# No row picking on TensorE in a graph layer's gather phase: GpSimd gathers all 46 rows of a round, and the histogram's operands get eight buffers

## The chip, the cores and the metric

One Trainium2 chip, one of its cores. The metric is the device time of one execution in microseconds (us), the median of the runs shown.

## What is computed

A graph layer followed by a mixture-of-experts feed-forward layer, both residual, on x of 6250 rows by 256 columns, in float32, with 200,000 edges sorted by their target node `dst`. Cut to the part that the change is in:

```
h    = batch_norm(layernorm(x) @ w1.T + b1)
diff = h[src] - h[dst]                    # 200,000 rows of 256
m    = segment_max(diff, dst)             # one row for each node
hg   = gelu(batch_norm(concat(h, m) @ wg.T + bg))
x    = x + batch_norm(hg @ w2.T + b2) + layernorm(x)
x    = x + experts(layernorm(x))          # 8 experts, three 256x256 layers each
```

Since `h[dst]` is the same for all edges of a node, `m` comes from the maximum of the gathered rows `h[src]` over each run of equal `dst`. So the middle of the kernel gathers 200,000 rows of 1 KB each and takes a running maximum over them.

## The kernel before

The edges are dealt out so that each of the 128 partitions holds 1564 consecutive edges. A step handles one edge of each partition, 128 rows; 46 steps make a round and 34 rounds make the gather phase. A round has seven groups of 7, 7, 7, 7, 6, 6 and 6 steps (`GS`). The rows of a round lie in `ring`, one slot for each step.

**The gather.** GpSimd (POOL) issues one indirect DMA for each step, line 648. Before each group it waits until the store of the same group of the round before has landed (`s_st`), and before every fourth gather until the running maximum is at most 21 steps behind (`s_ch`, `LEAD`). In rounds 1 to 32 it gathers 42 steps only (`by_pool`).

**The picks.** The last four steps of rounds 1 to 32 are made on TensorE (PE). The row numbers of the next round are broadcast to all partitions (SP, line 757, tile `ids`) and copied to PSUM (ACT, line 690). For each of 49 tiles of 128 nodes a one-hot matrix of 128 by 512 is built: four of seven by ScalarE (ACT) in two instructions (lines 670 and 675), three of seven by VectorE (DVE, line 821). PE multiplies the two halves of the node table, high and low part, with it: four matmuls of 512 columns (lines 999 and 1001). `picks_out`, `turn_back` and `result` turn the sum and write it into `ring[:, 42:46]`. Seven buffers `oh` hold the one-hot matrices; PE gives them back with `s_ohf`.

**The running maximum.** DVE does one instruction for each step, line 815, on `ring`, each waiting for the one before (`s_ch`). At a group's first step it waits for that group's gathers (`s_g`), at step 42 for the picks (`s_pe`). SP stores each finished group to `runs` (line 762).

**The histogram.** In rounds 0 to 31 each group also counts how many edges each node has: DVE builds two one-hot operands (`low_hots`, line 827, after the fourth step, and `high_hots`, line 832, after the fifth), and PE multiplies them in seven small matmuls (`counts`, line 970), the last of which increments `s_cnt`. There is one buffer of each operand, so `low_hots` first waits for the `counts` of the group before. The counts end with `s_c1`.

**Around it.** In rounds 0 to 15 SP also fetches pieces of the expert weights (`part`), ACT and DVE split them (lines 679 and 837), SP writes them back. Rounds 32 and 33 have no picks and no counts: there PE, ACT and DVE begin the first half of the second matmul (`columns`, line 1039, and `sums`, lines 189 to 191, 14 pieces; ACT takes them out in lines 724 and 730), while POOL and DVE finish the chain. DVE stops in round 32 after its first group for a product of PE (line 1059, read at line 911) and for what follows from the counts. The stage ends when the last of the 14 pieces is out.

Of the kernel before, what the change touches and what calls it, by code (L numbers as in the profile page):

```python
# [19 lines left out]
F32 = mybir.dt.float32  # L20
# [7 lines left out]
P = 128  # L28
N = 6250
C = 256  # L30
# [20 lines left out]
NPE = 4  # L51
PSLOT = STEPS - NPE
PG = ROUNDS - 2
SLOTS = 7
LEAD = 21
BD = (1, 3, 5)
BA = (0, 2, 4, 6)
# [15 lines left out]
assert NCH * TPC == NT and WIN * P >= E and (P - 1) * WIN < E and HR * HCOL >= WIN and HR == 4 * NE == PG and PG * NPE == P and SLOTS * NG == NT  # L73
# [23 lines left out]
def build(nc, io):  # L97
    ctx = ExitStack()
    with ctx:
# [15 lines left out]
        srcT_d = nc.dram_tensor("srcT_d", (PG, NPE * P), F32, kind="Internal").ap()  # L115
# [117 lines left out]
        places = sub(free0, ("zT", MAT), ("gT", 2 * MAT), ("ring", 0), ("src", WIN * 4), ("pen", WIN * 4), ("oh", SLOTS * NPE * P * 4),  # L233
# [28 lines left out]
        def h0_of(c):  # L262
# [7 lines left out]
        p2 = sub(places["free"], ("lo16", HR * HCOL * 2), ("hi16", HR * HCOL * 2), ("oh_lo", NG * P * 2), ("oh_hi", NG * NT * 2), ("ids", 2 * NPE * P * 4 + 512),  # L270
                 ("cnt", 6 * NT * 4), ("zr", P * 2), ("rowi", 2 * P * 4), ("rowf", 2 * P * 4), ("node", NT * 4), ("nodef", NT * 4),
                 ("nodeneg", NT * 4), ("fixi", 64), ("tri", P * 4), ("ones", P * 4))
        lo16 = plan.at("lo16", [P, HR * HCOL], BF16, p2["lo16"])
        hi16 = plan.at("hi16", [P, HR * HCOL], BF16, p2["hi16"])
        oh_lo = plan.at("oh_lo", [P, NG, P], BF16, p2["oh_lo"])
        oh_hi = plan.at("oh_hi", [P, NG, NT], BF16, p2["oh_hi"])
# [9 lines left out]
        nodef = plan.at("nodef", [P, NT], F32, p2["nodef"])  # L286
        nodeneg = plan.at("nodeneg", [P, NT], F32, p2["nodeneg"])
        dst_i = plan.at("dst_i", [P, WIN], I32, places["oh"])
        dig_i = plan.at("dig_i", [P, WIN], I32, places["part"])
        assert WIN * 4 <= SLOTS * NPE * P * 4 and WIN * 4 <= PW * 4 + 4096  # L290
# [5 lines left out]
        assert 6272 >= WIN * 4 and 6272 + 3 * C * 4 + P * 4 <= SLOTS * NPE * P * 4  # L296
# [277 lines left out]
        oh = plan.at("oh", [P, SLOTS, NPE * P], F32R, places["oh"])  # L574
        ids = plan.at("ids", [P, 2, NPE * P], F32, p2["ids"])
        srcf = plan.at("srcf", [P, PG * NPE], F32, places["part_hi"] + P * 4)
        part = plan.at("part", [P, PW], F32, places["part"])
        part_hi = plan.at("part_hi", [P, PW], F32R, places["part_hi"])
        srcTs = plan.at("srcTs", [P, P], F32, places["part"])
        accT = plan.at("accT", [P, KC, NPE * P], F32, places["part"] + PW * 4)  # L580
# [19 lines left out]
        s_ids, s_ch, s_oh, s_cnt = sem("s_ids"), sem("s_ch"), sem("s_oh"), sem("s_cnt")  # L600
        s_accS, s_back = sem("s_accS"), sem("s_back")
        s_ohd, s_oha, s_ohf, s_ab, s_pe, s_acc0, s_idp = sem("s_ohd"), sem("s_oha"), sem("s_ohf"), sem("s_ab"), sem("s_pe"), sem("s_acc0"), sem("s_idp")
        s_tt, s_tst, s_tev, s_zh, s_zl, s_srcf, s_srcT, s_srcS, s_srcD = sem("s_tt"), sem("s_tst"), sem("s_tev"), sem("s_zh"), sem("s_zl"), sem("s_srcf"), sem("s_srcT"), sem("s_srcS"), sem("s_srcD")
# [5 lines left out]
        ND, NA = NG * len(BD), NG * len(BA)  # L609
# [15 lines left out]
        def turned(n):  # L625

            return 4 if n < 2 else 2

        def by_pool(i, g):

            return GS[g] - (NPE if g == NG - 1 and 1 <= i <= PG else 0)

        def gathered(i, g):

            return 16 * sum(by_pool(j, g) for j in range(i + 1))

        with nc.Block() as block:

            @block.gpsimd
            def _(pool):  # L640
                for i in range(ROUNDS):
                    for g in range(NG):
                        if i:
                            pool.wait_ge(s_st[g], 16 * i)
                        for k in range(GO[g], GO[g] + by_pool(i, g)):
# [7 lines left out]
            def _(act):  # L653
                def picks_out(i):

                    two = (4, 2)[i % 2]
                    act.wait_ge(s_acc0, i + 1)
                    act.activation(accT[:].rearrange("p k n -> p (k n)"), banks(two, 2), ACT.Copy).then_inc(s_accS, 1)

                def result(i):  # L660

                    two = (4, 2)[(i - 1) % 2]
                    act.wait_ge(s_st[NG - 1], 16 * i)
                    act.wait_ge(s_ch, STEPS * i + 1)
                    act.wait_ge(s_back, i)
                    act.activation(ring[:, PSLOT:STEPS, :].rearrange("p s n -> p (s n)"), banks(two, 2), ACT.Copy).then_inc(s_pe, 1)

                def distance(i, h, g, v):
                    wait(act, s_ohf, NT * i + SLOTS * g + v + 1)
                    act.activation(oh[:, v, :], ids[:, bass.ds(h, 1), :].rearrange("p a n -> p (a n)"), ACT.Abs,  # L670
                                   bias=nodeneg[:, bass.ds(SLOTS * g + v, 1)]).then_inc(s_ab, 1)

                def one_hot(i, g, j, v):
                    wait(act, s_ab, NA * i + len(BA) * g + j + 1)
                    act.activation(oh[:, v, :], oh[:, v, :].bitcast(F32), ACT.Relu, bias=ones[:, 0:1], scale=-1.0).then_inc(s_oha, 1)  # L675

# [4 lines left out]
                def hots(i, h, g):  # L681
                    distance(i, h, g, BA[0])
                    for j in range(1, len(BA)):
                        distance(i, h, g, BA[j])
                        one_hot(i, g, j - 1, BA[j - 1])
                    one_hot(i, g, len(BA) - 1, BA[-1])
# [6 lines left out]
                def body(i, h, piece):  # L693
                    hots(i, h, 0)
                    if i:
                        picks_out(i - 1)
# [1293 lines left out]
```

## Time and profile before

| | |
|---|---|
| runs | 3648.39, 3649.25, 3667.12 us; median 3649.25 |
| span of the profiled execution | 3634.8 us; about 14 us of its time lie outside the span, if it ran as the median |
| gather phase, first gather's start to last gather's end | 98.7 to 2441.4 us |
| its last round, with 46 gathers | from 2382.2 us |
| end of the stage that follows it | 2524.7 us |

"Busy" is the time in which an engine executed an instruction. An idle time is put down to the instruction whose signal ended it; "remote" means that the signal came at a time that fits no recorded end of an instruction, and "issue" that no wait is to be seen. PEclk is the granted TensorE clock as a share of 2.4 GHz.

### The profile page before, as it was taken

What the parts mean: (1) busy time and instruction counts of PE and PEld (TensorE: products, weight loads), DVE (VectorE), ACT (ScalarE), POOL (GpSimd) and SP (SyncE); (2) the same over time, 40 slices, a digit from 0 to 9 for tenths busy, and PEclk for the clock granted to TensorE, in tenths of its full rate; (3) what the DMA queues carried; (4) which work ended last, traced back from release to release, by engine and by line L of the source; (5) the groups of instructions that cost most, each with busy time, mean ns of one, the idle gap of its engine ahead of it and who ended that gap; (6) DMA issues with size and microseconds to landing.
All of it is one profiled execution on the core that took longest, in us unless ns stands there. A gap on an engine that the chain in (4) does not pass through costs nothing. (4 is left out here: it accounts for less than half of the span.)

```text
span 3634.8 us, 41575 instructions
## 1 busy us (share of the span) xinstructions
PE 2966.5 (82%) x15504; PEld 2461.7 (68%) x15504; DVE 2207.0 (61%) x4089; ACT 1962.2 (54%) x2741; POOL 1496.1 (41%) x1530
## 2 busy tenths in 40 slices
PE   6578777787877778788887777728988999999998
PEld 5456565665665656566665666527878999999998
DVE  6576666666666666666666666540885556555544
ACT  5356555555555655555555555415165565566554
POOL 1566565565666655556665555561410000000000
PEclk9789898898898998889898898868999999999999
DMA  7355555555555555455555555450213324333331
GB/s 227 114 195 196 181 197 187 194 197 182 194 191 189 189 169 170 167 169 181 170 183 169 171 176 171 160 204 25 61 75 98 118 105 135 128 115 115 115 109 69
DMA packets 164927, 559.97 MB, mean 154 GB/s; under 512 B 31190, under 2 KB 68374, under 8 KB 157556
## 3 DMA queue, kind: packets, MB, share of 16 engines
q1 hardware_dynamic: 87492, 355.23, 26.1%
q0 software_dynamic: 77232, 202.08, 19.5%
q8 instruction: 122, 2.00, 0.2%
q14 instruction: 81, 0.66, 0.1%
HBM read 320.19 MB, written 237.00 MB: 153 GB/s over the span
## 5 line engine op out<-in xcount | busy, mean ns | idle before, releaser
L648 POOL DMA_INDIRECT ring<-runs,src_i x1436 | 1410.4, 982 | 1004.2 <-DVE ring L815 518.7
L999 PE MATMUL ps<-oh,zhl 128*128 128x512 f32 x3136 | 1347.5, 430 | 321.9 <-issue 159.7
L1001 PE MATMUL ps<-oh,zhl 128*128 128x512 f32 x3136 | 1308.0, 417 | 12.8 <-issue 12.5
L670 ACT ACTIVATE oh<-ids,nodeneg 128x512 fp32r<-128x512 f32 x896 | 633.6, 717 | 900.7 <-PE ps L1001 487.4
L999 PEld LDWEIGHTS ps<-oh,zhl 128*128 128x128 f32 x3136 | 642.1, 205 | 515.2 <-issue 186.4
L815 DVE SCALAR_TENSOR_TENSOR ring<-ring,pen 128x256 f32<-128x256 f32 x1564 | 750.4, 480 | 63.5 <-DMA ring<-runs,src_i 32.3
L821 DVE TENSOR_SCALAR oh<-ps,nodef 128x512 fp32r<-128x512 f32 x672 | 501.7, 747 | 403.6 <-PE ps L1001 248.5
L1001 PEld LDWEIGHTS ps<-oh,zhl 128*128 128x128 f32 x3136 | 643.2, 205 | 146.1 <-issue 15.3
L675 ACT ACTIVATE oh<-oh,ones 128x512 fp32r<-128x512 f32 x896 | 613.6, 709 | 0.0
L827 DVE TENSOR_TENSOR oh_lo<-lo,ps 128x896 bf16<-128x896 bf16 x224 | 242.8, 1084 | 328.7 <-remote 302.3
L1569 ACT ACTIVATE av<-ps,vecs 128x896 f32<-128x896 f32 x224 | 246.3, 1100 | 330.4 <-PE ps L191 330.4
L1717 DVE TENSOR_TENSOR h2l<-av,h2h 128x896 fp32r<-128x896 f32 x112 | 122.3, 1092 | 203.4 <-ACT h2h L1571 203.4
L1724 DVE SCALAR_TENSOR_TENSOR y<-ps,wv,y 128x256 f32<-128x256 f32 x392 | 168.9, 479 | 109.6 <-PE ps L1917 109.0
L1915 PE MATMUL ps<-fw,h2h 128*128 128x256 f32 x784 | 224.4, 286 | 3.3 <-DVE h2l L1717 3.3
L1916 PE MATMUL ps<-fw,h2l 128*128 128x256 f32 x784 | 221.8, 283 | 0.0
L1917 PE MATMUL ps<-fw,h2h 128*128 128x256 f32 x784 | 221.5, 282 | 0.0
L970 PE MATMUL ps<-oh_hi,oh_lo 128*128 128x49 bf16 x1575 | 85.4, 190 | 128.2 <-DVE oh_hi L832 69.4
L970 PEld LDWEIGHTS ps<-oh_hi,oh_lo 128*128 128x128 bf16 x1575 | 61.4, 99 | 180.6 <-issue 82.5
L1497 POOL DMA_DIRECT2D y<-in_x x5 | 8.4, 1671 | 415.6 <-DMA y<-res_d 415.6
L189 PE MATMUL ps<-h1h,fw 128*128 128x512 f32 x448 | 167.3, 374 | 1.9 <-DVE h1l L1717 1.9
L1717 DVE TENSOR_TENSOR h1l<-av,h1h 128x896 fp32r<-128x896 f32 x112 | 121.8, 1088 | 75.0 <-ACT h1h L1571 75.0
L191 PE MATMUL ps<-hnh,fw 128*128 128x512 f32 x448 | 164.6, 367 | 0.0
(294 smaller groups left out, 3872.2 us busy)
## 6 DMA issues: line engine op xcount, KB each, us to landing
runs<-ring SPq DMA_DIRECT2D x136, 896.0 KB
fw<-wsp SPq DMA_DIRECT2D x56, 1536.0 KB, 6.5
runs<-ring SPq DMA_DIRECT2D x102, 768.0 KB
ring<-runs,src_i POOLq DMA_INDIRECT x1436
ids<-srcT_d SPq DMA_DIRECT2D x32, 256.0 KB
res_d<-x_all SPq DMA_DIRECT2D x7, 896.0 KB
y<-res_d SPq DMA_DIRECT2D x7, 896.0 KB, 7.0
part<-in_Wx SPq DMA_DIRECT2D x16, 384.0 KB
```

What stands on the lines that cost most here:

```text
L648: pool.indirect_dma_start(ring[:, k, :], None, runs[0:N, :], bass.IndirectOffsetOnAxis(ap=src_i[:, STEPS * i + k:STEPS * i + k + 1], axis= ...
L670: act.activation(oh[:, v, :], ids[:, bass.ds(h, 1), :].rearrange("p a n -> p (a n)"), ACT.Abs, bias=nodeneg[:, bass.ds(SLOTS * g + v, 1)]) ...
L675: act.activation(oh[:, v, :], oh[:, v, :].bitcast(F32), ACT.Relu, bias=ones[:, 0:1], scale=-1.0).then_inc(s_oha, 1)
L815: dve.scalar_tensor_tensor(out=ring[:, k, :], in0=ring[:, before, :], scalar=pen[:, STEPS * i + k:STEPS * i + k + 1], in1=ring[:, k, :], o ...
L821: dve.tensor_scalar(oh[:, v, :], ps[:, bass.ds(6 + h, 1), :].rearrange("p a n -> p (a n)"), nodef[:, SLOTS * g + v:SLOTS * g + v + 1], Non ...
L827: dve.tensor_tensor(oh_lo[:], lo16[:, bass.ds(at, NG)].unsqueeze(2).to_broadcast([P, NG, P]), io_lo.unsqueeze(1).to_broadcast([P, NG, P]), ...
L999: pe.matmul(ps[:, two + k, :], z_hi(g)[:, v, cols], oh[:, v, :], start=g == 0 and v == 0, stop=False, skip_group_check=True)
L1001: r = pe.matmul(ps[:, two + k, :], z_lo(g)[:, v, cols], oh[:, v, :], start=False, stop=False, skip_group_check=True)
L1569: act.activation(av[:, m, :], block_banks(m), ACT.Relu, bias=dv(bi, 2 * e + m), scale=dv(sc, 2 * e + m)).then_inc(s_ev, 1)
L1717: dve.tensor_tensor(lo[:, m, :], av[:, m, :], hi[:, m, :].bitcast(F32), ALU.subtract).then_inc(s_hl6, 1)
L1915: pe.matmul(o, h2h[:, k, st], fw[:, b, 0, 2, k, :], start=k == 0, stop=False)
L1916: pe.matmul(o, h2l[:, k, st], fw[:, b, 0, 2, k, :], start=False, stop=False)
```

## The change

The picks are taken out: the one-hot matrices, the broadcast row numbers, their DMAs and semaphores, the copies into `ring`. POOL gathers 46 steps in every round. What PE still does in rounds 0 to 31 is `counts`. Their two operands have eight buffers, partly in the place of `oh` and `ids`: `low_hots` of group t waits for the `counts` of group t - 8. ACT's start on the following stage waits for `s_c1`, and so does SP's load of its weights (line 798 and its neighbour), which had waited for the last pick.

```
-NPE = 4
-PSLOT = STEPS - NPE
+NSET = 8
...
-        def by_pool(i, g):
-            return GS[g] - (NPE if g == NG - 1 and 1 <= i <= PG else 0)
...
                 def chain(i, k):
...
-                    if k == PSLOT and 1 <= i <= PG:
-                        dve.wait_ge(s_pe, i)
...
-                def one_hot(i, h, g, v):
-                    wait(dve, s_ohf, NT * i + SLOTS * g + v + 1)
-                    dve.tensor_scalar(oh[:, v, :], ps[:, bass.ds(6 + h, 1), :].rearrange("p a n -> p (a n)"),
-                                      nodef[:, SLOTS * g + v:SLOTS * g + v + 1], None, ALU.is_equal).then_inc(s_ohd, 1)
...
                 def low_hots(i, g):
-                    wait(dve, s_cnt, NG * i + g + 1)
+                    t = NG * i + g + 1
+                    if t >= NSET:
+                        wait(dve, s_cnt, t - NSET + 1)
...
                         if first:
                             row_low(g)
-                        chain(i, k)
-                        one_hot(i, h, g, BD[0])
-                        chain(i, k + 1)
-                        one_hot(i, h, g, BD[1])
-                        chain(i, k + 2)
-                        one_hot(i, h, g, BD[2])
-                        chain(i, k + 3)
+                        for j in range(4):
+                            chain(i, k + j)
                         low_hots(i, g)
...
-                for i in range(PG):
-                    picked(i)
-                counts(NG * HR)
-                turn_back(PG - 1)
+                for t in range(NG * HR + 1):
+                    counts(t)
...
-                rounds(body)
+                for i in range(2 * NE):
+                    high(i)
...
                 act.wait_ge(s_xs, 32 * 2 * NE)
+                act.wait_ge(s_c1, 1)
...
                 sp.wait_ge(s_xs, 32 * 2 * NE)
-                sp.wait_ge(s_acc0, PG)
+                sp.wait_ge(s_c1, 1)
```

## Rows read from the trace of the kernel before

**Rows 1.** The page, part 1: busy time, share, instructions of each engine.
```profile
PE 2966.5 (82%) x15504; PEld 2461.7 (68%) x15504; DVE 2207.0 (61%) x4089; ACT 1962.2 (54%) x2741; POOL 1496.1 (41%) x1530
```

**Rows 2.** Windows: round 0, rounds 1-31, round 32, round 33, PE's rest.
```profile
core 0: us, PE busy (x) PEld busy (x) DVE busy (x) ACT busy (x) POOL busy (x), PEclk, DMA share, GB/s
98.60:183.70 85.10, 50.75 (x235) 38.51 (x234) 55.35 (x110) 36.87 (x49) 48.46 (x46) 0.74 0.36 114
183.70:2303.10 2119.40, 1669.16 (x7890) 1290.39 (x7889) 1370.70 (x2526) 1198.87 (x1840) 1275.72 (x1302) 0.89 0.54 182
2303.10:2382.10 79.00, 53.55 (x247) 43.95 (x245) 39.77 (x90) 27.11 (x43) 40.77 (x42) 0.76 0.47 158
2382.10:2441.60 59.50, 9.02 (x32) 8.20 (x33) 27.97 (x58) 3.12 (x6) 45.48 (x46) 0.54 0.67 231
2441.60:2524.60 83.00, 75.02 (x424) 67.20 (x422) 2.91 (x6) 51.60 (x92) 0.00 (x0) 0.96 0.06 21
```

**Rows 3.** The gathers, line 648: durations, and what ended POOL's idle time.
```profile
L648 POOL DMA_INDIRECT ring<-runs,src_i x1436: 951/957/2510, 98.7 to 2440.4; - x180
...
  DVE ring L815: 518.7, 177
```

**Rows 4.** Waits in rounds 1 to 31: total, times, longest.
```profile
POOL ring L648 <- DVE ring L815: 464.8, 162, 6.1
...
DVE oh_lo L827 <- remote: 302.3, 63, 8.8
DVE oh L821 <- PE ps L1001: 239.4, 108, 9.4
```

**Rows 5.** Timeline around a pause of POOL: start, duration, engine, instruction, idle before.
```profile
895.92 0.34 PE L970 MATMUL ps<-oh_hi,oh_lo 128*128 128x49 bf16 x7
...
903.20 0.95 POOL L648 DMA_INDIRECT ring<-runs,src_i  x1 [0.30 <-issue]
906.53 1.09 DVE L827 TENSOR_TENSOR oh_lo<-lo,ps 128x896 bf16<-128x896 bf16 x1 [8.77 <-remote]
906.59 1.33 ACT L670 ACTIVATE oh<-ids,nodeneg 128x512 fp32r<-128x512 f32 x2 [4.89 <-remote]
...
910.11 0.95 POOL L648 DMA_INDIRECT ring<-runs,src_i  x1 [5.96 <-DVE ring L815]
```

**Rows 6.** The page, part 5: groups of instructions that the change removes.
```profile
L999 PE MATMUL ps<-oh,zhl 128*128 128x512 f32 x3136 | 1347.5, 430 | 321.9 <-issue 159.7
...
L670 ACT ACTIVATE oh<-ids,nodeneg 128x512 fp32r<-128x512 f32 x896 | 633.6, 717 | 900.7 <-PE ps L1001 487.4
...
L821 DVE TENSOR_SCALAR oh<-ps,nodef 128x512 fp32r<-128x512 f32 x672 | 501.7, 747 | 403.6 <-PE ps L1001 248.5
```

**Rows 7.** Timeline, DVE: a histogram pair, and the chain in round 33.
```profile
890.33 1.07 DVE L827 TENSOR_TENSOR oh_lo<-lo,ps 128x896 bf16<-128x896 bf16 x1
...
891.73 0.50 DVE L832 TENSOR_TENSOR oh_hi<-hi,ps 128x343 bf16<-128x343 bf16 x1
...
2411.77 3.63 DVE L815 SCALAR_TENSOR_TENSOR ring<-ring,pen 128x256 f32<-128x256 f32 x7 [5.22 <-DMA ring<-runs,src_i]
```

**Rows 8.** Timeline, DVE and POOL in round 32.
```profile
2359.86 0.16 DVE L911 TENSOR_TENSOR vecs<-vecs,ps 128x4 f32<-128x4 f32 x1 [22.44 <-PE ps L1059]
...
2369.13 1.08 POOL L648 DMA_INDIRECT ring<-runs,src_i  x1 [18.79 <-DVE ring L815]
```

**Rows 9.** Timeline, ACT in round 33: the next stage under unbroken gathers.
```profile
2390.55 1.09 ACT L724 ACTIVATE zs<-ps 128x512 fp32r<-128x512 f32 x2 [10.00 <-remote]
2402.50 0.58 ACT L730 ACTIVATE gT<-ps,vecs 128x384 f32<-128x384 f32 x1 [10.87 <-issue]
2419.99 0.58 ACT L730 ACTIVATE gT<-ps,vecs 128x384 f32<-128x384 f32 x1 [16.91 <-remote]
2436.82 0.87 ACT L724 ACTIVATE zs<-ps 128x384 fp32r<-128x384 f32 x2 [16.25 <-issue]
2448.08 1.05 ACT L730 ACTIVATE gT<-ps,vecs 128x384 f32<-128x384 f32 x2 [10.39 <-remote]
```

More of the change, by code:

```diff
@@ L623, in piece_of @@
             return n // 2, a, w
-        def turned(n):
-            return 4 if n < 2 else 2
-        def by_pool(i, g):
-            return GS[g] - (NPE if g == NG - 1 and 1 <= i <= PG else 0)
         def gathered(i, g):
-            return 16 * sum(by_pool(j, g) for j in range(i + 1))
+            return 16 * GS[g] * (i + 1)
         with nc.Block() as block:
@@ L644, in _ @@
                             pool.wait_ge(s_st[g], 16 * i)
-                        for k in range(GO[g], GO[g] + by_pool(i, g)):
+                        for k in range(GO[g], GO[g + 1]):
                             if (k - GO[g]) % 4 == 0 and STEPS * i + k > LEAD:
@@ L653, in _ @@
             def _(act):
[L654 to L675, printed above, removed]
                 def high(i):
@@ L679, in high @@
                     act.activation(part_hi[:], part[:], ACT.Copy).then_inc(s_xh, 1)
[L681 to L686, printed above, removed]
-                def numbers(i, h):
-                    wait(act, s_ids, 16 * i + 16)
-                    act.activation(ps[:, bass.ds(6 + h, 1), :].rearrange("p a n -> p (a n)"),
-                                   ids[:, bass.ds(h, 1), :].rearrange("p a n -> p (a n)"), ACT.Copy).then_inc(s_idp, 1)
[L693 to L696, printed above, removed]
-                    if i < PG - 1:
-                        if i:
-                            wait(act, s_ohd, ND * i)
-                        numbers(i + 1, 1 - h)
-                    hots(i, h, 1)
-                    if piece is not None:
-                        high(i)
-                    hots(i, h, 2)
-                    if i:
-                        result(i)
-                    for g in range(3, NG):
-                        hots(i, h, g)
-                act.wait_ge(s_srcT, 1)
-                act.activation(srcTs[:], ps[:, 6, 0:P], ACT.Copy).then_inc(s_srcS, 1)
                 for c in range(NCH):
@@ L775, in body @@
                 def body(i, h, piece):
-                    first = isinstance(i, int) and i == 0
-                    if not (isinstance(i, int) and i == PG - 1):
-                        wait(sp, s_ids, 16 * i + 16)
-                        if not first:
-                            wait(sp, s_oha, NA * i)
-                        columns(i + 1, 1 - h)
                     if piece is not None:
@@ L866, in body @@
                     first = isinstance(i, int) and i == 0
-                    wait(dve, s_idp, i + 1)
                     for g in range(NG):
```

107 lines of the change are left out of this document (23 added, 84 removed).

## The prediction

> **What bounds the kernel now.** I read the page first: PE is busy for 82% of the span [rows 1], which would make the picks the thing to remove. But a share over the whole span says little, so I next asked for windows by round. Rounds 1 to 31 take 2119.4 us, 68.4 us each. In them PE is busy 1669 us of 2119, DVE 1371, ACT 1199, POOL 1276 [rows 2]: four engines at 57 to 79%, none of them full. Such a stretch is bound by how they wait for each other, and so the third view was the waits. The reader is to see a ring in it: POOL waits 465 us for the running maximum, and DVE waits 302 us before `low_hots` and 239 us before its one-hot matrices [rows 4], both for signals of PE.
>
> The fourth view, the timeline around one such wait, shows that PE is not late with its work. The seven matmuls of `counts` start at 895.92 and take 0.34 us in all. DVE, which needs nothing but their signal, starts at 906.53, ten us later, and so does ACT at 906.59. What happened between is that POOL, after a row of back-to-back gathers, ended its last one at 904.15 and stood still [rows 5]. I read this as: while POOL issues gathers without a break, signals of PE come late, and when POOL stops they all come, 2.4 us later in these rows. POOL then waits on for DVE's next steps, 5.96 us in all, and the circle begins again. A place without picks shows the same. In round 33 POOL gathers 46 times in 59.5 us without a pause [rows 2], and ACT, which takes out sums that PE has long finished, gets its signals one at a time at 2390.55, 2402.50, 2419.99, 2436.82 and, with POOL done at 2441.4, the next at 2448.08 [rows 9]. From 2390.55 to 2436.82 these are three intervals of 15.4 us on the mean; with the waits of 10.00 and 10.39 us at both ends, about 13.5 to 14 us.
>
> So the gather phase is bound by POOL's gathers plus the pauses in which PE's signals catch up. 42 gathers at 1275.72 / 1302 = 0.980 us, with 0.30 us between two of them [rows 2, 5], make 53.8 us; the other 14.6 us of a round are pauses: POOL's waits for DVE alone are 464.8 / 31 = 15.0 us a round, the longest 6.1 us [rows 4].
>
> **What is removed.** 3136 matmuls of line 999 and as many of line 1001, 896 distances and 896 one-hots on ACT, 672 one-hots on DVE [rows 6], the turning back, the broadcast of the row numbers on SP. None of this is paid for on POOL, so its 1348 us of PE or 502 us of DVE are no terms of the sum. What it is worth is that DVE and ACT no longer wait for PE 49 times in a round.
>
> **What is added.** Four gathers in each of 32 rounds. For the cost of a round of 46 there is a direct measurement, round 33: 59.5 us with 46 chain steps and seven stores beside them, DMA share 0.67 [rows 2]. The other end is the median gather, 46 x (0.957 + 0.30) = 57.8 us [rows 3, 5]. I take 59.5, since there DVE works beside it as it will; 57.8 would be worth another 53 us over 31 rounds.
>
> DVE does not become the bound: seven chain steps take 3.63 us, a histogram pair 1.07 and 0.50 us [rows 7]. A round is 46 x 0.52 + 7 x 1.57 = 35 us of 59.5. Nor does the DMA: in round 33 DVE waits 5.2 us for a group's gathers and then has 3.6 us of work [rows 7], 8.9 us for 7 steps, which is POOL's pace; POOL waits for no landing at all. Stores hold nothing up either: the view of [rows 4] has no wait of POOL for one, and with POOL at most 24 of 46 steps ahead a group's store has 15 steps, about 19 us, to land. SP loses work and gains none.
>
> **Eight buffers.** `low_hots` still needs PE's signal, now that of eight groups back. A group lasts 59.5 x 7 / 46 = 9.05 us, so the signal may be 7 x 9.05 = 63 us late. PE gives one signal in 9.05 us; if unbroken gathers let through one in 14 us [rows 9], the queue grows by 1/9.05 - 1/14 = 0.039 a us and reaches seven after about 180 us. From then on DVE goes at one group in 14 us, POOL at one in 9.05; POOL has about 12 steps of its 21 to spare and loses 3.8 in each group, so it pauses some 45 us later. The pause is that of [rows 5], 6 us: the signals all come, DVE makes four steps, POOL goes on. That is 6 us in each 230, in rounds 1 to 31 eight pauses, 48 us. The ends: nothing, if the queue is emptied in time after all; and one pause after each seven groups and the 12 spare steps, 63 + 15 us and the pause itself, every 84 us, if unbroken gathers let nothing through: 22 pauses, 132 us. I take 48, because [rows 9] is the only stretch with the new pace, and things went through there.
>
> The Trainium skill (TensorE: Matmul & The Clock Gate, "The cost: per-tile semaphore tail") gives 26.3 ns for each increment. By it the signals would never be late, the eight buffers would be worth nothing, and the sum would have 0 here. The ten us in [rows 5] are against it; the time it gives is the first rival's.
>
> **The sum**, on the span. Round 0: DVE's chain of it starts when the statistics before it are done, which the change doesn't touch; POOL waits for that as before. DVE saves its 21 one-hots, POOL's own 46 gathers stay: 82 for 85.1. Rounds 1 to 31: 31 x 59.5 = 1844.5 for 2119.4. Round 32: four gathers more, 5 us, on 79.0 [rows 2]. Its pause of 18.79 us [rows 8] stays, since DVE waits for a product of PE that POOL's gathers delay; SP loads the weights for it only after `s_c1` now, which was not so, but the signal comes in the pause as before. 84. Round 33: 59.5. Pauses: 48. Together 2118 for 2343.1, that is 225 us less. What follows (83.0 us, PE busy 75 of them [rows 2]) keeps its length: the pieces that PE could finish during rounds 32 and 33 are held up by the gathers now as before. The profiled span is 3634.8, the median 3649.25, about 14 us outside it that stay: 3649 - 225 = 3424.
>
> **Rivals.** *No pauses* (chance 0.20): one signal in 9 us gets through. For it: even now, with PE sending eight signals in each group, DVE was held for a late one at `low_hots` 63 times in 217 groups [rows 4], not each time. Against: [rows 9], where one came in 14 us. It gives 3649 - 273 = 3376, and with the fast gathers 3325.
>
> *Nothing gets through* (0.15): 22 pauses of 6 us, 3649 - 273 + 132 = 3508; if the signals take the 6.7 us to come that they took after POOL's last gather [rows 9], a pause is 10 us and the time 3596.
>
> *Slower than before* (0.04): DVE's chain holds up POOL's descriptor work. The chain's instruction has both inputs in SBUF, and if POOL stood still for all of its 0.48 us, a round would be 57.8 + 46 x 0.48 = 80 us, 31 x (80 - 68.4) = 360 us more than before, some 4010 us; it ends slower from 68.4 us a round on, that is when 0.23 us of each chain step hold POOL up. The Trainium skill (SBUF — State Buffer, "Who interferes with whom") says that a DVE instruction with two SBUF inputs and a GpSimd instruction that reads SBUF block each other fully. Round 33 is against it: 46 chain steps, and the 46 gathers beside them took 45.48 us, 0.989 each against the median of 0.957 [rows 2, 3], so 0.03 us of a step, not 0.48.
>
> *No change* (0.02): the pauses stay as they are, 14.6 us a round, and the four gathers add 5 us, which the shorter round 0 does not pay; this would need DVE to wait for each `counts` signal, which eight buffers exclude as long as a signal is under 63 us late.
>
> My own case has 0.59, with a range of its own of 3375 to 3470. The range for 8 in 10 goes from the middle of the first rival to the middle of the second: 3345 to 3520. Faster by over 0.5% (18 us, about what a measurement of this kernel can tell): 0.94; within 0.5%: 0.02; slower: 0.04.
>
> **What the profile after should show.** 1564 gathers, mean 0.98 to 0.99 us. Rounds 1 to 31 of 60 to 62 us. POOL's waits for DVE in these rounds, 465 us before, at 40 to 60, in few pieces of 3 to 6 us each, one in about four rounds, and before each of them DVE waiting at `low_hots` for 10 us or more for a signal of PE that was finished long ago. DVE waiting 4 to 6 us in each group for gathers. PE's granted clock mostly at the lower of its levels, 1.2 GHz, as in round 33 (0.54 of 2.4 GHz [rows 2]). A gather phase of about 2118 us, the stage after it 83 us as before.
>
> **What would make this wrong.** If DVE's waits at `low_hots` are gone, the first rival holds and the time is below 3400. If they come once or twice in a round, the second. If gathers take over 1.1 us with DVE busy, the third. If round 32's pause grows beyond 19 us, because `s_c1` stands behind up to seven late signals and the load of the weights and ACT's work behind it, the time is up to 20 us above the sum.

## The result and the profile after

The changed kernel takes 3532.84 us, the median of four runs (3531.34 to 3536.09), against 3648.82 us before (four runs, 3645.08 to 3667.12). The ratio is 0.9685, with a 95% interval of 0.966 to 0.971: 3.2% faster. I had predicted 3424 us, a gain of 225; the gain is 116, about half, and the time lies 13 us above my range. The profiled execution took 3531.3 us with a span of 3529.6, 105 less than before.

The engines' busy times, from the page, to be laid beside [rows 1]:

```profile
PE 1400.1 (40%) x8911; PEld 1223.8 (35%) x8911; DVE 1811.5 (51%) x3414; ACT 733.2 (21%) x852; POOL 1632.1 (46%) x1658
```

1566 us of PE's busy time and 1229 of ACT's are gone, and the span gave back 105. The windows by stage, to be laid beside [rows 2]: round 0, rounds 1 to 31, round 32, round 33, and what PE still does after.

```profile
core 0: us, PE busy (x) PEld busy (x) DVE busy (x) ACT busy (x) POOL busy (x), PEclk, DMA share, GB/s
97.60:180.00 82.40, 23.80 (x131) 17.03 (x130) 53.33 (x101) 11.72 (x10) 50.81 (x46) 0.56 0.38 121
180.00:2196.90 2016.90, 158.16 (x1533) 96.61 (x1533) 994.22 (x1889) 12.64 (x15) 1406.54 (x1426) 0.50 0.59 195
2196.90:2277.70 80.80, 23.29 (x112) 20.47 (x113) 29.05 (x71) 10.06 (x18) 45.07 (x46) 0.56 0.48 158
2277.70:2336.80 59.10, 10.37 (x34) 8.57 (x32) 22.49 (x46) 2.61 (x5) 44.94 (x46) 0.56 0.64 212
2336.80:2420.00 83.20, 74.23 (x418) 66.80 (x418) 2.91 (x6) 50.99 (x91) 0.00 (x0) 0.92 0.05 20
```

Four of the five rows are within 3.2 us of their terms (82, 84, 59.5, 83). All of the miss is in one: rounds 1 to 31 take 2016.9 us, 65.1 a round, where 1844.5 + 48 = 1892.5 were forecast. The gathers are not to blame; line 627, the view of one line:

```profile
L627 POOL DMA_INDIRECT ring<-runs,src_i x1564: 947/953/2697, 97.6 to 2335.5; - x196
```

The median is 953 ns and the mean in rounds 1 to 31 1406.5 / 1426 = 0.986 us. So POOL was busy for 1406.5 us, 1426 x 0.30 = 428 is the step from one gather to the next [rows 5], and the remaining 182 us are pauses. I had 48 on top of 59.5 us a round, and on that base it is 2016.9 - 1844.5 = 172. The waits of these rounds, to be laid beside [rows 4], show their shape:

```profile
POOL ring L627 <- issue: 414.8, 1296, 3.8
DVE ring L722 <- remote: 315.2, 170, 3.1
...
DVE oh_lo L731 <- remote: 200.4, 25, 15.1
DVE ring L722 <- issue: 173.2, 115, 7.0
DVE ring L722 <- DMA ring<-runs,src_i: 151.1, 42, 6.6
POOL ring L627 <- DVE ring L722: 134.7, 105, 8.7
DVE ring L722 <- DVE ring L722: 132.0, 177, 1.3
POOL ring L627 <- remote: 60.9, 25, 4.2
```

POOL's waits for DVE and for signals of no known origin are 134.7 + 60.9 = 196 us, where I had forecast 40 to 60. DVE still waits at `low_hots` (`oh_lo`, line 731), 25 times, up to 15.1 us; the one signal that this line of the kernel waits for is PE's. New is the running maximum, line 722: it waits for its own step before, hundreds of times and up to 3.1 us, where the chain of [rows 7] had a step each 0.52 us. DVE's timeline in two stretches, before and after signals began to come late (a line with x4 is four steps in a row):

```profile
227.44 2.11 DVE L722 SCALAR_TENSOR_TENSOR ring<-ring,pen 128x256 f32<-128x256 f32 x4
229.46 1.08 DVE L731 TENSOR_TENSOR oh_lo<-lo,ps 128x896 bf16<-128x896 bf16 x1
...
324.26 0.48 DVE L722 SCALAR_TENSOR_TENSOR ring<-ring,pen 128x256 f32<-128x256 f32 x1 [0.85 <-DVE ring L722]
325.66 0.48 DVE L722 SCALAR_TENSOR_TENSOR ring<-ring,pen 128x256 f32<-128x256 f32 x1 [0.92 <-DVE ring L722]
327.06 0.48 DVE L722 SCALAR_TENSOR_TENSOR ring<-ring,pen 128x256 f32<-128x256 f32 x1 [0.92 <-DVE ring L722]
327.46 1.08 DVE L731 TENSOR_TENSOR oh_lo<-lo,ps 128x896 bf16<-128x896 bf16 x1
...
333.44 0.48 DVE L722 SCALAR_TENSOR_TENSOR ring<-ring,pen 128x256 f32<-128x256 f32 x1 [2.39 <-remote]
335.46 0.48 DVE L722 SCALAR_TENSOR_TENSOR ring<-ring,pen 128x256 f32<-128x256 f32 x1 [1.54 <-remote]
```

In the second stretch a step of 0.48 us comes every 1.4 us and more. `low_hots` at 327.46, which needs nothing of the step before, starts 0.40 us after that step: instructions reach DVE in time, and only what waits for the step before is late. DVE falls behind, and POOL, which looks before every fourth gather whether it is at most 21 steps ahead, stands still for it:

```profile
327.30 1.08 POOL L627 DMA_INDIRECT ring<-runs,src_i  x1 [2.50 <-DVE ring L722]
...
334.09 0.95 POOL L627 DMA_INDIRECT ring<-runs,src_i  x1 [3.06 <-remote]
```

In round 32 POOL's one pause, for the chain that DVE had left [rows 8], is now 22.05 us, where it was 18.79; the round is still 3 us shorter than I had it.

### The profile page after: what moved, and what is told of

Its sections match the earlier page's. It is cut to its first block and busy times, and to the rows that moved or that the text cites. A ratio compares the mean times of both kernels' runs of the same rounds, so it can differ in the third digit from the quotient of the medians.

```text
span 3529.6 us, 25757 instructions
## 1 busy us (share of the span) xinstructions
PE 1400.1 (40%) x8911; PEld 1223.8 (35%) x8911; DVE 1811.5 (51%) x3414; ACT 733.2 (21%) x852; POOL 1632.1 (46%) x1658
## 5 line engine op out<-in xcount | busy, mean ns | idle before, releaser
L627 POOL DMA_INDIRECT ring<-runs,src_i x1564 | 1547.4, 989 | 763.5 <-issue 454.1
L864 PE MATMUL ps<-oh_hi,oh_lo 128*128 128x49 bf16 x1575 | 160.9, 214 | 1903.5 <-issue 1302.0
L864 PEld LDWEIGHTS ps<-oh_hi,oh_lo 128*128 128x128 bf16 x1575 | 98.6, 113 | 1965.8 <-issue 1345.2
L649 ACT ACTIVATE zs<-ps 128x512 fp32r<-128x512 f32 (+1 forms) x56 | 27.4, 541 | 1177.0 <-remote 1166.3
L635 ACT ACTIVATE part_hi<-part 128x768 fp32r<-128x768 f32 x16 | 13.5, 842 | 945.2 <-DMA part<-in_Wx 762.8
L184 PE MATMUL ps<-h1h,fw 128*128 128x512 f32 x448 | 167.4, 374 | 1.9 <-DVE h1l L1570 1.9
L185 PE MATMUL ps<-hnl,fw 128*128 128x512 f32 x448 | 164.5, 367 | 0.0
L186 PE MATMUL ps<-hnh,fw 128*128 128x512 f32 x448 | 164.4, 367 | 0.0
L186 PE MATMUL ps<-h1h,fw 128*128 128x512 f32 x448 | 164.0, 366 | 0.0
L185 PE MATMUL ps<-h1l,fw 128*128 128x512 f32 x448 | 163.7, 365 | 0.0
L184 PE MATMUL ps<-hnh,fw 128*128 128x512 f32 x448 | 163.5, 365 | 0.0
L1768 PEld LDWEIGHTS ps<-fw,h2h 128*128 128x128 f32 x784 | 150.8, 192 | 4.3 <-DVE h2l L1570 3.7
```

Source lines behind the costliest of these rows:

```text
L184: pe.matmul(out, wh, xh, start=first and i == 0, stop=False)
L185: pe.matmul(out, wh, xl, start=False, stop=False)
L186: r = pe.matmul(out, wl, xh, start=False, stop=last and i == n - 1)
L627: pool.indirect_dma_start(ring[:, k, :], None, runs[0:N, :], bass.IndirectOffsetOnAxis(ap=src_i[:, STEPS * i + k:STEPS * i + k + 1], axis= ...
L864: r = pe.matmul(ps[:, 0, 0:NT], oh_lo[t % NSET][:, n, :], oh_hi[t % NSET][:, n, :], start=False, stop=False, skip_group_check=True)
L1768: pe.matmul(o, h2h[:, k, st], fw[:, b, 0, 2, k, :], start=k == 0, stop=False)
```

## The experiments

All times are medians of four or more runs, beside runs of the kernel before on the same chip. That matters here, since the 18 experiments fell on six chips, and the kernel before is not the same on them: 3077.7, 3081.7 and 3079.3 us on three of them (called 3080 chips below), 3639.9, 3593.9 and 3651.0 on the other three (3640 chips; the result above, 3648.8, is of their kind). Some edits ran on both kinds; each repeat has a label of its own.

**Four kernels that each undo or lighten a part (e1 to e4).** e1 has one buffer for the histogram's operands:

```
-NSET = 8
+NSET = 1
```

> The kernel after with one buffer for the histogram's operands in place of eight, so only the picks are taken out. Theory A (signals are late while POOL gathers without a break, and eight buffers absorb part of that): DVE stands at low_hots in nearly each group until POOL has paused, some 15 us of pauses on 59.5 us a round as before, 31 x (74 - 65) = 280 us more than the 3533 us of the kernel after, about 3800. Rival B (the buffers are worth nothing, taking the picks out is the whole gain): 3533.

e2 is the kernel before, picks kept, with two buffers (eight don't fit beside the picks' tiles):

```
+        NSET = 2
...
-                    wait(dve, s_cnt, NG * i + g + 1)
+                    t = NG * i + g + 1
+                    if t >= NSET:
+                        wait(dve, s_cnt, t - NSET + 1)
```

> The kernel before with two buffers for the histogram's operands in place of one, picks kept (there is no room for more beside them). Theory A: low_hots waits no longer (302 us of waits in the kernel before), but DVE's and ACT's one-hot matrices wait for the same late signals of PE right behind it, so the pauses stay: 3600 to 3649. Rival C (the buffers carry the gain and the picks cost nothing): 3530 to 3560.

e3 is the changed kernel without `counts` on PE, so it leaves out the histogram, and without DVE's wait for it:

```
-                    if t >= NSET:
-                        wait(dve, s_cnt, t - NSET + 1)
...
-                for t in range(NG * HR + 1):
-                    counts(t)
+                wait(pe, s_oh, NG * HR + 1)
```

> The kernel after without the histogram's matmuls: TensorE stands still from round 0 to the end of round 31 and sends no signal; DVE still builds the operands. It leaves out the run-end histogram. Theory A (besides PE's signals also DVE's own come late, so its chain, which waits for its own signal at each step, falls behind): the waits at low_hots go, the slow stretches of the chain stay, only the pauses of over 5 us go, some 50 us in all: about 3480. Rival D (only PE's late signals make pauses): rounds 1 to 31 at 59.5 us, 172 us less, 3361.

e4 has PE signal in each fourth group only; DVE's wait, not shown, counts in fours with it:

```
-                    r.then_inc(s_cnt, 1)
+                    if t % 4 == 3:
+                        r.then_inc(s_cnt, 1)
```

> The kernel after with TensorE signalling only each fourth group of the histogram, eight buffers kept. Theory A with a rate (unbroken gathers let one PE signal through in about 14 us, and one is sent in 36 us here): as with TensorE silent, 3480 to 3500. Rival E (signals are held until POOL pauses, however few they are): DVE stands as often as in the kernel after or oftener, 3533 or more. Rival D: 3361.

All four fell on a 3080 chip, with the kernel before at 3077.7 us, and all my expectations had been written for the other kind. e1 took 3234.0 us (ratio 1.051, interval 1.049 to 1.053), e3 3233.4 (1.050, 1.049 to 1.052), e4 3233.0 (1.050, 1.048 to 1.052), e2 3079.2 (1.001, 1.000 to 1.002). So here every kernel without the picks is 5% slower than the one with them, and neither the buffers nor PE's signals change anything beyond the intervals. Rounds 1 to 31 by windows, first of e4, then of e2 with its 42 gathers:

```profile
166.30:2001.90 1835.60, 103.13 (x1526) 73.65 (x1526) 978.07 (x1877) 12.63 (x15) 1400.91 (x1426) 0.50 0.64 214
```

```profile
164.00:1852.60 1688.60, 1553.80 (x7951) 1230.13 (x7951) 1355.25 (x2542) 1218.33 (x1853) 1291.80 (x1302) 0.96 0.69 229
```

That is 1835.6 / 1426 = 1.287 us for a gather and 1688.6 / 1302 = 1.297: POOL's busy time and 0.30 us between gathers leave 7 and 6 us of these stretches, so the round is POOL's gathers and nothing else, with the picks or without. The transfers are no slower on a 3640 chip: the mean busy time of the DMA engines is 0.64 x 1835.6 = 1175 us in e4 and 0.59 x 2016.9 = 1190 us in the changed kernel. PE makes all its picks in the 54.5 us that POOL needs for 42 gathers. POOL's longest wait in e4 is the ordinary one:

```profile
POOL ring L627 <- issue: 377.4, 1238, 0.3
POOL ring L627 <- DVE ring L722: 57.3, 188, 0.3
```

Taking the picks out therefore costs four gathers a round, 1835.6 - 1688.6 = 147 us of the 3233.0 - 3079.2 = 154 between the two.

**The changed kernel again, and three more (e5 to e8).** They fell on a 3640 chip, the kernel before at 3639.9 us. e5 has no edit.

> The changed kernel, nothing edited. Theory A: it was faster than the kernel before because signals come late while GpSimd gathers without a break, and how late they come is a property of the chip that runs it. Then its time follows the kernel before beside it: if the kernel before takes about 3078 us here, as in the four runs before this one, the changed kernel takes 3225 to 3240 us (ratio about 1.05, no pause of GpSimd in rounds 1 to 31, 58 to 61 us a round); if the kernel before takes about 3649 us, 3520 to 3545 us (0.968, some 66 pauses). Theory B: the four edits tried so far each cost it the same 5%, and the unchanged one is faster than the kernel before on any chip: under 3040 us beside 3078.

3534.0 us, ratio 0.971 (0.967 to 0.975), as in the result. The changed kernel without an edit was never run on a 3080 chip; four variants of it were (e1, e3, e4, e16; e1 and e3 again as e9 and e12), and take 3231 to 3238 us there.

e6 orders the chain by a drain of DVE's pipe, not by its own signal:

```
                     if STEPS * i + k:
-                        dve.wait_ge(s_ch, STEPS * i + k)
+                        dve.drain()
```

> VectorE's chain waits for the previous step by a drain of its own pipe in place of a wait for its own semaphore. Theory A (VectorE's own signals come late after some 60 unbroken gathers): on a chip where the kernel before takes 3649 us, chain steps stay 0.5 us apart, GpSimd no longer pauses for the chain but only where a late signal of TensorE holds VectorE, and rounds 1 to 31 take 60 to 62 us each for 65.1, about 3400 to 3440 us in all. Theory C (the chain is slow since its instructions compete with the gathers for SBUF): the steps stay 1.3 to 3.5 us apart and the time stays 3530. On a chip where the kernel before takes 3078 us nothing is late, so within 10 us of the unchanged kernel by both.

3531.5 us, ratio 0.971 (0.967 to 0.975): nothing. And the steps are as far apart as before, though none waits for a signal; DVE's timeline of e6:

```profile
324.17 0.48 DVE L722 SCALAR_TENSOR_TENSOR ring<-ring,pen 128x256 f32<-128x256 f32 x1 [1.89 <-issue]
325.57 0.48 DVE L722 SCALAR_TENSOR_TENSOR ring<-ring,pen 128x256 f32<-128x256 f32 x1 [0.92 <-issue]
327.65 0.48 DVE L722 SCALAR_TENSOR_TENSOR ring<-ring,pen 128x256 f32<-128x256 f32 x1 [1.60 <-issue]
```

The same 0.92 us stands in front of a step in both kernels. So the chain's own semaphore is not what is late; the step before counts as done late for its successor, whichever way that is asked. Theory A falls in this part. Competition for SBUF (theory C) does not explain it either: the instruction itself keeps its 0.48 us, and in e16 on a 3080 chip the same drains, beside gathers at a faster pace, give four steps in 2.16 us:

```profile
322.37 2.16 DVE L726 SCALAR_TENSOR_TENSOR ring<-ring,pen 128x256 f32<-128x256 f32 x4 [2.93 <-DMA ring<-runs,src_i]
```

e7 stops POOL twice in a round:

```
                                                     ).then_inc(s_g[g], 16)
+                        if g in (2, 6):
+                            pool.wait_ge(s_g[g], gathered(i, g))
```

> GpSimd waits twice in each round, after the third and the seventh group, until that group's own gathers have landed; nothing else is changed. Theory A: with a stop in each 26 us no row of gathers is long enough for signals to fall behind; each stop costs the landing time of the last gather, some 2 us, so 4 us a round. Where the kernel before takes 3649 us: rounds 1 to 31 take 62 to 64 us each, in which all pauses are these stops, in all 3440 to 3510 us, under the unchanged kernel's 3533. Where it takes 3078 us: 4 us a round more than the unchanged kernel, about 3360 us. Theory C: the stops only add, in both cases 100 to 140 us above the unchanged kernel.

3535.2 us, ratio 0.971 (0.967 to 0.976), a round of 2042.9 / 31 = 65.9 us. With the stops nothing is late any more: the view of DVE's waits in rounds 1 to 31 has no line for `low_hots` and none for the step before, only the gathers, and POOL's view has the stops.

```profile
DVE ring L724 <- DMA ring<-runs,src_i: 1011.8, 211, 7.3
DVE ring L724 <- issue: 18.9, 6, 4.5
...
POOL ring L627 <- issue: 427.0, 1310, 5.0
POOL ring L627 <- DMA ring<-runs,src_i: 197.2, 56, 4.4
```

And the time is the same. I had expected either a gain of some 20 to 90 us or a loss of 100 to 140; the stops took the place of the pauses. They last 197.2 / 56 = 3.5 us on the mean. By itself e7 doesn't tell a fixed pace of gathers from a stop that cures the lateness and costs as much: at the 2 us that a stop costs on a 3080 chip (e11 below), its 62 stops would be 124 of its 2042.9 - 1400.4 - 428 = 215 us of pauses.

e8 leaves out one gather in each of four groups, from round 1 on, so POOL issues 42 in a round and no picks are made (those steps work on old rows):

```
+                            if i and g < 4 and k == GO[g + 1] - 1:
+                                continue
```

> Leaves out one gather in each of the first four groups of rounds 1 to 33, the steps then working on rows left from the round before; everything else is that of the changed kernel, so GpSimd issues 42 gathers in a round as the kernel before does, and TensorE picks no rows. Theory A: a gather costs 1.29 us of a round where nothing is late, so with 4 fewer a round takes 54 to 55 us and the whole 33 x 5.1 = 170 us less than the unchanged kernel: about 3065 us where the kernel before takes 3078, that is, the same within 0.6%, since what TensorE and VectorE save there is worth nothing. Theory D (the picks' work cost the kernel before something too, hidden under the same round time): under 3030 us. Where the kernel before takes 3649 us: about 3350 us.

3348.6 us, ratio 0.920 (0.916 to 0.924). Rounds 1 to 31:

```profile
180.50:2024.70 1844.20, 159.60 (x1533) 96.87 (x1533) 993.02 (x1889) 12.64 (x15) 1290.54 (x1302) 0.50 0.60 205
```

1844.2 / 1302 = 1.416 us for a gather; in the changed kernel it was 2016.9 / 1426 = 1.414. This pair splits the change on a 3640 chip: e8 is 3639.9 - 3348.6 = 291 us under the kernel before, and the changed kernel is 3534.0 - 3348.6 = 185 us over e8, 1.40 us for each of 132 gathers. Four of these are in round 33, where the kernel before gathers 46 as well; with them set apart (4 x 1.40 = 6 us, an estimate), taking out the picks, with eight buffers, is worth some 285 us, and the 128 gathers that make up for them take some 180 of it back.

**Meant for a 3640 chip (e9 to e12).** e9, e10 and e12 are e1, e2 and e3 once more; e11 stops POOL once a round (`if g == 6:`).

> The changed kernel with one buffer for the histogram's operands in place of eight, once more, since the first run of it fell on a chip without late signals. Theory A (late signals cost by the pause they make GpSimd take, and pauses come when signals have fallen behind after some 60 gathers, whoever waits): where the kernel before takes about 3640 us, VectorE waits at the low digits' one-hots 217 times for a signal one group old, up to 10 us late, so it is late for GpSimd in nearly each round as in the kernel before: 68 to 70 us a round of 46, about 3620 to 3690 us. Theory F (the eight buffers are worth nothing even there, as the rate is set elsewhere, 1.415 us for each gather in rounds 1 to 31 of both the changed kernel and the one with 42 gathers): 3525 to 3545 us. Where the kernel before takes 3078 us: 3234 us again.

> The kernel before, picks kept, with two buffers for the histogram's operands, once more. Where the kernel before takes about 3640 us: by theory A the signal at the low digits' one-hots may now be one group (9 us) late, but VectorE still waits for TensorE's distances some 28 times a round, so 3560 to 3640 us. By theory F a round of 42 gathers takes 42 x 1.415 = 59.4 us and what the kernel before takes beyond that (68.4) is all due to the picks' waits, so no difference: within 0.5% of the kernel before. Where the kernel before takes 3078 us: the same again.

> GpSimd waits once a round, after the last group, for its gathers to land, where e7 had it wait twice and the unchanged kernel not at all. Theory A: a stop costs the 3.4 to 3.7 us that it cost in e7, and one in 46 gathers is enough to keep the signals in time, since late ones were seen only after some 60. Then a round takes 57.8 + 3.6 = 61.4 to 62.5 us, and where the kernel before takes about 3640 us the whole takes 3410 to 3460 us, under the unchanged kernel's 3534. Theory G (the chip takes gathers at 1.415 us each and no faster over a long time, and the stop only moves where the backlog is waited for): the stop grows to about 7 us, a round stays at 65 us, 3525 to 3560 us. Where the kernel before takes 3078 us: 2 us a round more than the unchanged kernel, about 3290 us.

> Leaves out the run-end histogram on TensorE, so VectorE waits for no signal of TensorE in rounds 1 to 31, once more. Theory A as I predicted it (pauses come from TensorE's late signals alone): where the kernel before takes about 3640 us, no pauses are left, 3360 to 3390 us. Theory H (VectorE's own signals, each step of the chain waiting for the one before, are late as well, and the signals that GpSimd waits for): the pauses stay, 3500 to 3540 us. Theory G: 3525 to 3540 us. Where the kernel before takes 3078 us: 3233 us again.

They fell on a 3080 chip, the kernel before at 3081.7 us: 3237.7 us (1.052, 1.050 to 1.053), 3080.0 (1.000, 0.999 to 1.001), 3300.5 (1.071, 1.069 to 1.073) and 3234.1 (1.050, 1.048 to 1.052). The first, second and last repeat the earlier ones. The stop costs 2 us a round there, 66 us in all beside e12; nothing was there for it to clear, and POOL's waits for its gathers are shorter than in e7, 76.9 / 32 = 2.4 us:

```profile
POOL ring L627 <- DMA ring<-runs,src_i: 76.9, 32, 4.2
```

So e10 leaves open what two buffers would do to the kernel before on a 3640 chip.

**The same on a 3640 chip (e13 to e15)**: e11, e9 and e12 again.

> One stop of GpSimd in each round, after its last group, until the gathers have landed; the second run. On a chip where the kernel before takes 3078 us it cost 2.1 us a round (3300 us). Where it takes about 3640 us: theory A (unbroken gathering makes signals late, a stop of 3.6 us clears it) 61.4 to 62.5 us a round, 3410 to 3460 us. Theory G (1.415 us a gather is what that chip keeps over a long time) 65 us a round, 3525 to 3560 us.

> One buffer for the histogram's operands; the third run. Where the kernel before takes about 3640 us: theory A 68 to 70 us a round, 3620 to 3690 us; theory F (the buffers are worth nothing, the pace of 1.415 us a gather sets the round) 3525 to 3545 us. Where it takes 3078 us: 3235 us.

> Leaves out the run-end histogram on TensorE; the third run. Where the kernel before takes about 3640 us: theory A as predicted (TensorE's late signals alone make the pauses) 3360 to 3390 us; theory H (VectorE's own are late as well) and theory G 3500 to 3540 us. Where it takes 3078 us: 3233 us.

The kernel before took 3593.9 us. With one stop: 3513.9 us (0.979, 0.975 to 0.983). With one buffer: 3533.6 (0.982, 0.979 to 0.985). Without the histogram: 3501.5 (0.974, 0.971 to 0.977). The changed kernel without an edit did not run on this chip. What counts in each is the window of its rounds 1 to 31; in the order e13, e14, e15:

```profile
184.10:2187.30 2003.20, 145.37 (x1489) 89.91 (x1488) 982.98 (x1868) 12.64 (x15) 1402.81 (x1426) 0.50 0.59 196
```

```profile
180.70:2206.80 2026.10, 102.66 (x1519) 73.19 (x1519) 984.10 (x1877) 12.64 (x15) 1407.67 (x1426) 0.50 0.58 194
```

```profile
181.30:2172.00 1990.70, 0.00 (x0) 0.00 (x0) 986.53 (x1871) 12.64 (x15) 1421.21 (x1426) 0.50 0.59 197
```

That is 1.405, 1.421 and 1.396 us for a gather. Where DVE is held is quite different: with one buffer it waits 604 us at `low_hots` and hardly at all for a step of the chain, without PE's signals it waits 462 + 250 us inside the chain. DVE's waits, of e14 and of e15:

```profile
DVE oh_lo L732 <- remote: 603.9, 59, 15.1
...
DVE ring L723 <- DVE ring L723: 1.8, 4, 0.5
```

```profile
DVE ring L722 <- remote: 461.5, 262, 3.1
DVE ring L722 <- DVE ring L722: 250.3, 360, 1.6
```

The pauses of POOL, worked out as above, are 173, 191 and 142 us, for 182 in the changed kernel on its chip. Of e13's 173, the stops are about a third (31 x 2 = 62, by e11's price), and the others remain: one stop in 46 gathers neither prevents the lateness nor lengthens the round. That is what tells a pace from theory A, which had late signals only after some 60 gathers. e13 shows one thing more. Its stop ends after 2.03 us, so the gathers had landed promptly, and seven us later DVE's steps are 3 us late (the timelines of POOL and DVE):

```profile
369.70 0.95 POOL L627 DMA_INDIRECT ring<-runs,src_i  x1 [2.03 <-DMA ring<-runs,src_i]
...
371.99 0.48 DVE L724 SCALAR_TENSOR_TENSOR ring<-ring,pen 128x256 f32<-128x256 f32 x1 [1.63 <-remote]
...
376.88 0.48 DVE L724 SCALAR_TENSOR_TENSOR ring<-ring,pen 128x256 f32<-128x256 f32 x1 [2.95 <-remote]
```

Whatever has filled up there (that something fills up is my picture, and no row shows it), it is not the gathers' data on their way, and a stop of 2 us does not empty it; of e7's longer stops, 1.1 us more than on a 3080 chip, this can't be said.

**Fewer signals, smaller gathers (e16 to e18).** e16 and e18 are one kernel: a drain in the chain, the signal of e4, and

```
-                                             op0=ALU.add, op1=ALU.max).then_inc(s_ch, 1)
+                                             op0=ALU.add, op1=ALU.max)
+                    if k + 1 in GO:
+                        r.then_inc(s_ch, 1)
```

with the waits of POOL and SP counted in groups. e17 gathers 64 rows from round 1 on (`ring[0:64, k, :]`, `src_i[0:64, ...]`); the other 64 partitions work on old rows.

> Nothing of the work is left out. VectorE's chain follows its own pipe by a drain, and gives a signal after each group only, 7 a round in place of 46; TensorE gives one in each four groups. Theory J (what runs full are the engines' signals themselves, as e15 hints at 0.07 us each): some 1370 signals fewer, 90 us less than the unchanged kernel where the kernel before takes about 3600 us, 3420 to 3460 us. Theory K (the gathers' own descriptors or completions fill it, the signals only stand in it): 3500 to 3540 us. Where the kernel before takes 3078 us: within 15 us of 3233.

> From round 1 on each gather fetches 64 rows in place of 128, so half of the descriptors and of the bytes; the other 64 partitions work on what was there (this changes the result). Where the kernel before takes about 3600 us: theory K, descriptors fill it: no signal is late any more, and rounds 1 to 31 take what GpSimd's issuing takes, which is under 58 us, shorter if a gather of 64 rows is issued in less than 0.957 us; at the same issue time 3350 us or less, with no pause of GpSimd over 0.6 us. Theory J, signals or completions (as many as before): pauses of 140 us or more stay in rounds 1 to 31. Where the kernel before takes 3078 us it tells only what 64 rows cost GpSimd to issue: 3233 us if the cost is per instruction, 2950 us if a third of it is by row.

> VectorE's chain with a drain and a signal after each group only, TensorE's signal in each fourth group; no work left out. Where the kernel before takes about 3600 us: theory J 3420 to 3460 us, theory K 3500 to 3540 us. Where it takes 3078 us: 3231 us again.

e16 and e17 fell on a 3080 chip (3079.3 us before): 3231.4 us (1.049, 1.048 to 1.051) and 3168.2 (1.029, 1.027 to 1.031). A gather of 64 rows keeps POOL busy for 0.941 us where one of 128 took 0.984 in e1: the cost of an issue there is almost all per instruction. e18 fell on a 3640 chip (3651.0 before): 3552.8 us, ratio 0.973 (0.969 to 0.977). The kernel gives some 1370 signals fewer in rounds 1 to 31, and POOL's pauses are 191 us: theory J falls. Whether the gathers' descriptors are what fills up (theory K) would need e17 on a 3640 chip; that was not tried.

## Why the prediction was wrong

**The step that failed** is in the part on the eight buffers: "That is 6 us in each 230, in rounds 1 to 31 eight pauses, 48 us." On the base of that sum it was 172 us, counted from POOL's own busy time and steps 182. I had taken the pause to be the end of a chain of delays that starts with a late signal of PE, and counted how long eight buffers could ride it out. The 3640 chips show another rule. In the changed kernel as it is, with one buffer, without PE's signals, with far fewer signals of DVE and PE, with one stop in each round or two, rounds 1 to 31 take 1.40 to 1.43 us for each gather; and with 42 gathers 1.42. The 3080 chips take 1.29 to 1.30, with full gathers and no stops. POOL may run at 1.26 us for a round or two (the best rounds of the changed kernel are 58.1 to 59.9 us), and each time it is made to stand still later, until the mean is near 1.41. That POOL is held to a mean pace is how I read these eight kernels; it is argued from their agreement, not shown by a run that sets the pace. If POOL doesn't stop by itself, completions on the other engines come late until it must; if it is stopped by hand, part of the pauses are these stops. The size of the pauses is thus a term of its own: 1426 x (1.414 - 1.286) = 182 us, in proportion to the gathers, which the change made more.

**Round 33, on which I leaned, was too short.** 46 gathers in 59.5 us without a pause [rows 2] was a true row and a poor sample: such rounds exist in the changed kernel too, and they are paid for in the next one or two (rounds 2 and 3 take 59.5 and 72.2 us).

**"DVE does not become the bound"** was worked out from steps of 0.52 us. In the late stretches the steps are 1.4 to 3 us apart; DVE's work was as small as forecast, 994 us of 2017, its completions were not.

**The rival "nothing gets through"** gave 132 us of pauses and 3508 us and is the nearest in size, but it counted 22 pauses of 6 us at `low_hots`, and with e15, where no signal of PE is left, 142 us of pauses are still there, for 173 (e13) and 191 (e14) on the same chip. PE's and the histogram's part is some 30 to 50.

**The slower side.** My chance for slower was 0.04, and for one mechanism, the chain holding up POOL's descriptor work. That mechanism did not come: a gather beside DVE's chain takes 0.986 us. On a 3080 chip every variant of the change that gathers all rows and has no stop is slower by 5%, for the reason that I had booked and thought small, four gathers a round; what is missing there is the 285 us to be gained. The profile of before could not show this. It did show, though, that the gain rested wholly on pauses that no record explained.

**The kernel before** takes 2119.4 / 1302 = 1.63 us for a gather [rows 2], 0.21 above the 1.416 of e8. These 2119.4 - 1844.2 = 275 us go with the picks, as e8 shows, and that pauses would go with them was predicted rightly. That I had put the gain in rounds 1 to 31 at 2119.4 - 1844.5 = 275 us too is chance: mine was to be left after four more gathers a round were paid. How the picks make these pauses was not tested apart from taking them out.

**The eight buffers** bear nothing that can be seen: 3234.0 us with one and 3233.0 with eight on one 3080 chip, 3533.6 with one on a 3640 chip, 3532.8 and 3534.0 with eight on others of that kind. On a 3640 chip one buffer and eight were not run side by side.

**The terms.** "About 14 us outside it": the profiled execution of the changed kernel takes only 1.7 us more than its span; if that held before too, its execution took 3636.6 us, less than the median. This made the sum 12 us too high and hid a tenth of the error. PE's clock was 0.50 of 2.4 GHz in rounds 1 to 31, as forecast, and cost nothing, with PE busy for 158 us of 2017. Round 32 took 80.8 us for 84, though its pause grew.

**The working.** Three of its figures don't follow from its own terms. The interval between ACT's signals, with the waits at both ends, is (46.27 + 20.39) / 5 = 13.3 us, not 13.5 to 14. The first rival with the fast gathers is 3376 - 53 = 3323, not 3325. And the middle of the second rival, between its ends 3508 and 3596, is 3552, not 3520; a range made as I said would have held the measured time, by luck and not by its mechanism.

The Trainium skill (TensorE: Matmul & The Clock Gate, "The cost: per-tile semaphore tail") has 26.3 ns for each semaphore increment of a matmul tile. On the 3080 chips nothing contradicts it: no wait of POOL is over 0.3 us in e4. On the 3640 chips DVE waits up to 15.1 us for a signal of PE, and a step of DVE counts as done late even where no semaphore is waited for (e6), so no price for each increment would describe it. The Trainium skill's rule that a DVE instruction with two SBUF inputs and a GpSimd instruction that reads SBUF block each other (SBUF — State Buffer, "Who interferes with whom") is not borne out for the issue of an indirect DMA, if that counts as such an instruction: a full block would put the chain's 46 x 0.48 = 22 us on top of a round's 57.8 us of gathers, and e4's round takes 1835.6 / 31 = 59.2.

**Left open**: what holds gathers to one in 1.41 us, whether their descriptors, their completions or something else, and why three of six chips don't have it.

## What to carry to other kernels

A pause that nothing in the profile explains is not to be priced as if the one wait that shows it were its cause. Divide the stretch by the number of the bounding engine's instructions, kernel by kernel: 1.40 to 1.43 us for each gather in eight kernels showed what no single wait did, that further buffers, stops or fewer signals all give next to nothing. One kernel is not enough for it; the kernel before alone has 1.63, and 1.29 in its last round.

Work moved onto the engine that sets the pace was paid in full each time, 1.29 us a gather on a 3080 chip and 1.40 on a 3640 chip, and what it relieves may be free elsewhere. Where a kernel's gain rests on such pauses, measure both kernels on more than one chip before keeping it: 3% faster on two chips, with variants 2 to 3% faster on two more, and variants 5% slower on three others is a choice about machines, not about kernels.

## What the runs showed of the hardware

On the six chips of the experiments the kernel before takes 3078 to 3082 us or 3594 to 3651, with nothing between, and the instructions themselves take the same time: in rounds 1 to 31 POOL is busy for 1401 us on a 3080 chip (e4) and 1407 us in the result, DVE for 978 and 994.

While POOL issues indirect DMAs without a break on a 3640 chip, completions of DVE and PE become visible late, DVE's own to itself, with a semaphore or with a drain alike (steps of 0.48 us come 1.4 to 3 us apart). A stop for a gather's landing lasted 2.03 us in such a stretch of e13; in e7 it lasted 3.5 on the mean, against 2.4 in e11 on a 3080 chip.

A stop of POOL for the landing of its last gather costs 2 us a round on a 3080 chip (e11), and half the rows in a gather make its issue only 4% cheaper there (e17).
